# Attention scores: six bf16 part products on 99 rows, or fp32r halves in two 64-row tiles

## What is computed

```python
h = _layernorm(x) * (1 + ca) + sa
q = (h @ Wq.T); k = (h @ Wk.T); v = (h @ Wv.T)     # 32 query heads, 8 key/value heads, 16 wide
q = q * cos + _rotate_half(q) * sin; k = k * cos + _rotate_half(k) * sin
scores = einsum('bhgtd,bhkd->bhgtk', q, k) / sqrt(16)
scores = where(causal, scores, finfo.min)
attn = softmax(scores); ctx = einsum('bhgtk,bhkd->bhgtd', attn, v)
```

## Time and profile before

| | us |
|---|---|
| three runs | 859.87, 862.03 (median), 863.3 |
| the profiled execution | 858.42 |
| its span, first to last instruction | 856.4 |
| PE, DVE, ACT, POOL busy in it | 751.3, 494.3, 322.4, 217.8 |
| first score product, first transposed scores, first output projection work | 65.6, 111.7, 388 |
| one head of the loop (from one `mod_step` to the next) | 35.74 |

### The profile page before, as it was taken

The page is one execution under the profiler, slowest core; times in us unless marked ns, Lnnn a source line. Parts: engine busy times, 40 slices in busy tenths (PEclk is TensorE's granted clock), DMA queues, the critical chain, the costliest instruction groups (busy, mean ns, idle before and its releaser), DMA issues.

```text
span 856.4 us, 11611 instructions
## 1 busy us (share of the span) xinstructions
PE 751.3 (88%) x3950; PEld 462.8 (54%) x3950; DVE 494.3 (58%) x726; ACT 322.4 (38%) x533; POOL 217.8 (25%) x167
## 2 busy tenths in 40 slices
PE   3678599999999999989979999887778899997998
PEld 1565233343333433217658888644346688885886
DVE  5858876767667676406845537793686423336310
ACT  6121046555665556762315511254213322332100
POOL 2546461200000000161236523231323122222500
PEclk9789789999999999999989999998779899999999
DMA  9057893610010101211013300110221011111110
GB/s 319 10 117 104 162 181 114 81 64 21 42 63 0 63 21 42 90 38 62 2 25 102 106 1 1 33 59 1 38 65 36 25 50 49 49 35 39 62 62 37
DMA packets 24377, 52.88 MB, mean 62 GB/s; under 512 B 4017, under 2 KB 8857, under 8 KB 23321
## 3 DMA queue, kind: packets, MB, share of 16 engines
q1 hardware_dynamic: 24345, 52.46, 23.6%
HBM read 45.63 MB, written 6.62 MB: 61 GB/s over the span
## 4 chain that ended last, share of the span: by engine, by line
PE 74%; DVE 14%; issue 5%; ACT 3%; DMA 2%; POOL 2%; SPq 1%; ACTq 0%; DVEq 0%; POOLq 0%
PE ps L843 72%; DVE mxp L1716 3%; DVE xnb L1599 1%; ACT pr L1406 1%; PE ps L860 1%; DVE arena L1611 1%; DVE arena L1608 1%; DMA wm<-in_wm 1%; DVE st L1577 1%; PE ps L1002 1%; DMA Qst<-mparts 1%; DVE dg L1947 1%; DVE rt L1905 1%; POOL rs L2068 0%; POOL hrs L2252 0%
## 5 line engine op out<-in xcount | busy, mean ns | idle before, releaser
L843 PE MATMUL ps<-arena 128*128 128x512 f32 (+1 forms) x1560 | 373.2, 400 | 26.2 <-DVE arena L1611 18.3
L843 PEld LDWEIGHTS ps<-arena 128*128 128x128 f32 (+1 forms) x1560 | 296.4, 191 | 95.4 <-DVE arena L1611 25.6
L1716 DVE TENSOR_REDUCE mxp<-ps 128x2 f32<-128x1024 f32 (+3 forms) x160 | 173.1, 1116 | 68.5 <-PE ps L843 67.5
L1406 ACT ACTIVATE pr<-ps 128x512 f32<-128x512 f32 x288 | 161.7, 596 | 124.7 <-PE ps L843 122.1
L843 PE MATMUL ps<-Kst,Qst 96*128 (+4 forms) x384 | 102.1, 338 | 11.9 <-DVE full L1736 6.0
L843 PE MATMUL ps<-Qst,Kst 99*128 (+1 forms) x288 | 105.1, 386 | 8.2 <-ACT pr L1406 4.3
L843 PE MATMUL ps<-pr,vr 128*32 128x512 f32 x576 | 76.7, 605 | 0.7 <-ACT pr L1406 0.7
L843 PEld LDWEIGHTS ps<-Kst,Qst 96*128 (+1 forms) x384 | 36.1, 100 | 75.4 <-issue 34.0
L843 PE MATMUL ps<-maskb,identb 128*128 128x128 bf16 (+1 forms) x320 | 75.0, 257 | 0.0
L843 PEld LDWEIGHTS ps<-Qst,Kst 99*128 (+1 forms) x288 | 27.1, 97 | 77.3 <-ACT pr L1406 49.8
L2151 POOL COPY vr<-vtok 128x128 f32 (+1 forms) x8 | 2.3, 292 | 205.4 <-PE ps L843 205.4
(11 more groups left out here) (187 smaller groups left out, 779.3 us busy)
## 6 DMA issues: line engine op xcount, KB each, us to landing
wmr<-in_wmr SPq DMA_DIRECT2D x8, 1280.0 KB, 5.8
raw<-in_w SPq DMA_DIRECT2D x16, 512.0 KB, 3.3
Qst<-q_parts SPq DMA_DIRECT2D x18, 256.0 KB, 8.8
q_parts<-qparts SPq DMA_DIRECT2D x3, 768.0 KB, 8.5
x<-in_x SPq DMA_DIRECT2D x8, 256.0 KB, 6.1
wm<-in_wm SPq DMA_DIRECT2D x4, 512.0 KB, 7.0
raw<-in_up SPq DMA_DIRECT2D x8, 256.0 KB, 2.7
raw<-in_down SPq DMA_DIRECT2D x8, 256.0 KB, 2.6
```

The lines of the kernel that those rows point to most:

```text
L843: return nc.tensor.matmul(outp, lhs, rhs, start=start, stop=stop, skip_group_check=True)
L1406: A(pr[:, k % PRING, :], ps[:, 4 + k % 2, :], ACT.Exp, scale=float(DH) ** -0.5).then_inc(exp_done, 1)
L1716: V.tensor_reduce(mxp[:, kh, g0:g0 + heads, i].rearrange("p (b e) -> p b e", e=per), units, AXX, ALU.max)\
```

## The change

The scores are computed from fp32r halves. A stack holds hi·hi, hi·lo and lo·hi, 48 rows of 16 each. Plain scores read rows 64 to 111 of the new `Qst` and `Kst`, transposed scores rows 0 to 49 (48 and two rows of minus the maxima, as fp32r halves). The two kinds thus lie in different 64-row tiles of PE's array. Stacks are held for two heads instead of eight, and SP streams them: per head five DMAs into the upper rows and five into the lower. Loops over heads are unrolled. A unit is issued product by product (`s_piece`) among the transposed units, and ahead of `pv_round` where it stood behind. Masks are two 64-row bf16 products for a bank instead of one 128-row product for a block. Projections are plain fp32 from unsplit operands (`h0T`, `wkv`, `wq`): one product instruction a chunk instead of three. Five jobs come before the first scores; five (`FILL`) in halves behind units 0 to 9 of head 0, two later.

```diff
-KROWS = 6 * DH
+SROWS, TROWS = 3 * DH, 3 * DH + 2
+S0 = 64
...
+FILL = (("v", 1), ("q", 1, 0), ("q", 1, 1), ("q", 2, 0), ("q", 2, 1))
+VT_AT = 11
...
+    def unit(d, s):
+        heads = SUNITS[s][2]
+        for e in range(heads):
+            todo.append(("s", d, (s, e), reduce_cost(s) / heads))
...
-        Qst = at("Qst", [99, NKV, G, T], BF16, ACT_B)
-        Kst = at("Kst", [99, NKV, T], BF16, ACT_B + 65536)
+        Qst = at("Qst", [P, 2, G, T], F32R, ACT_B)
+        Kst = at("Kst", [P, 2, T], F32R, ACT_B + 32768)
...
+        maskb = at("maskb", [P, 5, 64], BF16, ACT_B + 81920 + 7168)
+        h0T = at("h0T", [P, KC, T], F32, ACT_B + 40 * 1024)
+        wq = at("wq", [P, KC, D], F32, ACT_B + 56 * 1024)
...
+        qsw = [at(f"qsw{c}", [P, T], F32, WR_B + (12 + 4 * c) * 1024)[:, :] for c in range(1, 4)]
+        qacc = at("qacc", [P, T], F32, WR_B + 28 * 1024)
+        qparts = at("qparts", [P, 2, T], F32R, WR_B + 40 * 1024)
...
+            def load_keys(base, n, tok_, done):
+                s = n % 2
+                sp.dma_start(Kst[base:base + 2 * DH, s, tok_].bitcast(F32), kscr[:, DH * n:DH * n + DH, tok_]).then_inc(done, 16)
+                sp.dma_start(Kst[base + 2 * DH:base + 3 * DH, s, tok_].bitcast(F32), kscr[0, DH * n:DH * n + DH, tok_]).then_inc(done, 16)
+            def load_queries(base, n, tok_, done):
+                s = n % 2
+                r = G * DH * (n % 2)
+                hi, lo = [qscr[n // 2, q, r:r + G * DH, tok_].rearrange("(g d) t -> d g t", d=DH) for q in range(2)]
+                for k in range(2):
+                    sp.dma_start(Qst[base + DH * k:base + DH * k + DH, s, :, tok_].bitcast(F32), hi).then_inc(done, 16)
+                sp.dma_start(Qst[base + 2 * DH:base + 3 * DH, s, :, tok_].bitcast(F32), lo).then_inc(done, 16)
+            every = slice(0, T)
+            sp.wait_ge(kst_ones, 1)
             for hf in range(2):
-                for n in (2 * hf, 2 * hf + 1):
-                    store_parts(n)
-                stored(2 * hf)
-                load_keys(0, 2, tok[hf], k_in[hf])
-                stored(2 * hf + 1)
-                load_queries(0, tok[hf], q0_in[hf])
-            load_keys(2, NKV, slice(0, T), k_rest)
-            def later_queries(c):
-                sp.wait_ge(part_q, c)
-                sp.dma_start(qscr[c, :, :, :].rearrange("q p t -> p q t"), qparts[:, :, :]).then_inc(q_out, 16)
-                sp.wait_ge(q_out, 16 * c)
-                load_queries(c, slice(0, T), q_in[c])
-            filled(sp, ("q", 3, 1))
-            sp.dma_start(wmr[:, :, :].rearrange("p c n -> p (c n)"), a["wmr"][0]).then_inc(wmr_in, 16)
-            later_queries(1)
-            def head_dmas(h, more):
+                sp.wait_ge(k_lo, hf + 1)
+                sp.dma_start(kscr[:, :, tok[hf]].rearrange("q p t -> p q t"), parts[2 * hf][:, :, :].bitcast(F32)).then_inc(part_out[2 * hf], 16)
+                sp.wait_ge(q_lo, hf + 1)
+                sp.dma_start(qscr[0, :, :, tok[hf]].rearrange("q p t -> p q t"), parts[2 * hf + 1][:, :, :].bitcast(F32))\
+                    .then_inc(part_out[2 * hf + 1], 16)
+                sp.wait_ge(part_out[2 * hf], 16)
+                load_keys(S0, 0, tok[hf], s0_in[hf])
+                sp.wait_ge(part_out[2 * hf + 1], 16)
+                load_queries(S0, 0, tok[hf], s0_in[hf])
+            for n in range(2):
+                if n:
+                    load_keys(S0, n, every, s_in[n])
+                    load_queries(S0, n, every, s_in[n])
+                load_keys(0, n, every, t_in[n])
+                load_queries(0, n, every, t_in[n])
...
+            for h in range(NKV):
+                head_dmas(h)
+                if h < 3:
+                    sp.wait_ge(part_q, h + 1)
+                    sp.dma_start(qscr[h + 1, :, :, :].rearrange("q p t -> p q t"), qparts[:, :, :].bitcast(F32)).then_inc(q_out, 16)
+                if h < NKV - 2:
+                    sp.wait_ge(q_out, 16 * ((h + 2) // 2))
+                    load_keys(S0, h + 2, every, s_in[h % 2])
+                    load_queries(S0, h + 2, every, s_in[h % 2])
+                if 1 <= h < NKV - 1:
+                    sp.wait_ge(t_full, h * NTU)
+                    load_keys(0, h + 1, every, t_in[(h + 1) % 2])
+                    load_queries(0, h + 1, every, t_in[(h + 1) % 2])
...
+            def project(name, hf, w, fresh=False, chunks=range(KC)):
+                b = bank_of(pe, name) if chunks[0] == 0 else banks.get(name)[0]
+                for kc in chunks:
+                    if fresh:
+                        evacuated(pe, ("ln", 0, hf, kc))
+                    last = mm(ps[:, b, :], w[:, kc, :], h0T[:, kc, tok[hf]], kc == 0, kc == KC - 1)
+                if chunks[-1] == KC - 1:
+                    last.then_inc(full_b[b], 1)
...
+            pe.wait_ge(wkv_in, 16)
             keys(0)
+            pe.wait_ge(wq_sorted, KC)
+            queries(0, 0)
             ln_turn(0, 1)
-            values(0)
-            weights(pe, ("wqkv", 1))
-            queries(0, 0)
-            ln_split(pe, 0, 1)
             keys(1)
             queries(0, 1)
-            values(1)
-            queries(1, 0)
-            queries(1, 1)
-            queries(2, 0)
-            def s_unit(h, s):
+            values(0)
...
+            Z = maskb[:, 0:3, :].rearrange("p a b -> p (a b)")
+            low, all_low = maskb[:, 3, :], maskb[:, 3:5, :].rearrange("p a b -> p (a b)")
+            def s_piece(h, s, e):
                 slot = s % 2
                 i, g0, heads, kh = SUNITS[s]
                 w = width(i, kh)
-                before = slots_before(h, s)
-                if not isinstance(before, int) or before >= 2:
-                    pe.wait_ge(s_read, before - 1)
+                if e == 0:
+                    before = slots_before(h, s)
+                    if before >= 2:
+                        pe.wait_ge(s_read, before - 1)
                 diag = kh == (0 if i < 4 else 1)
                 per = min(heads, 512 // w)
-                for e in range(heads):
-                    o = ps[:, 2 * slot + e // per, w * (e % per):w * (e % per) + w]
-                    last = mm(o, Qst[0:KROWS, bass.ds(h, 1), g0 + e, i * P:(i + 1) * P]
-                              .rearrange("p n t -> p (n t)"),
-                              Kst[0:KROWS, bass.ds(h, 1), 512 * kh:512 * kh + w].rearrange("p n t -> p (n t)"),
-                              True, not diag)
-                    if diag:
-                        last = mm(o[:, w - P:w], identb[:, :], maskb[:, 0, :], False, True)
-                last.then_inc(s_full, 1)
+                b = 2 * slot + e // per
+                last = mm(ps[:, b, w * (e % per):w * (e % per) + w],
+                          Qst[S0:S0 + SROWS, h % 2, g0 + e, i * P:(i + 1) * P],
+                          Kst[S0:S0 + SROWS, h % 2, 512 * kh:512 * kh + w], e % per == 0, not diag)
+                if diag and e % per == per - 1:
+                    o = ps[:, b, 0:per * w].rearrange("p (e w) -> p e w", w=w)
+                    mm(o[:, :, w - P:w], Z[S0:P, 64:192], all_low[S0:P, :].unsqueeze(1).to_broadcast([64, per, P]),
+                       False, False)
+                    last = mm(o[:, :, w - 64:w], Z[S0:P, 0:P], low[S0:P, :].unsqueeze(1).to_broadcast([64, per, 64]),
+                              False, True)
+                if e == heads - 1:
+                    last.then_inc(s_full, 1)
+            def s_unit(h, s):
+                for e in range(SUNITS[s][2]):
...
+                    pe.wait_ge(t_in[n % 2], 80 * (n // 2 + 1))
+                    pe.wait_ge(mrow_in, 32 * n + 32)
+                if k >= 2 or n > 0:
                     pe.wait_ge(exp_done, n * NTU + k - 1)
                 o = ps[:, 4 + k % 2, :].rearrange("p (g t) -> p g t", g=G)
-                last = mm(o, Kst[:, bass.ds(n, 1), j * P:(j + 1) * P].rearrange("p n t -> p (n t)"),
-                          Qst[:, bass.ds(n, 1), :, i * P:(i + 1) * P].rearrange("p n g t -> p (n g) t"),
-                          True, i > j)
+                last = mm(o, Kst[0:TROWS, n % 2, j * P:(j + 1) * P], Qst[0:TROWS, n % 2, :, i * P:(i + 1) * P], True, i > j)
                 if i == j:
-                    last = mm(o, identb[:, :], maskb[:, 1, :].unsqueeze(1).to_broadcast([P, G, P]), False, True)
+                    mm(o[:, :, 0:64], Z[0:64, 64:192], maskb[0:64, 4, :].unsqueeze(1).to_broadcast([64, G, 64]), False, False)
+                    last = mm(o, Z[0:64, 0:P], all_low[0:64, :].unsqueeze(1).to_broadcast([64, G, P]), False, True)
                 last.then_inc(t_full, 1)
...
+            pe.wait_ge(s0_in[0], 80)
             for s in range(NS):
                 if s == LATER:
-                    queries(2, 1)
+                    pe.wait_ge(s0_in[1], 80)
+                s_unit(0, s)
+                if s < 2 * len(FILL):
+                    job, half = FILL[s // 2], range(2 * (s % 2), 2 * (s % 2) + 2)
+                    if job[0] == "v":
```

(38 more changed lines are left out.)

400 lines of the change are left out of this document (148 added, 252 removed).

## The result

| | kernel before | changed kernel |
|---|---|---|
| median of the runs, us | 862.18 (859.87 to 863.3) | 946.42 (943.04 to 974.14) |
| ratio, 95% interval | | 1.0966 (1.0932 to 1.1) |
| profiled execution, span us | 856.4 | 944.6 |
| granted clock over the span | 0.944 | 0.873 |

A forecast was written before the change was run, and what follows sets the result against it. PE was taken to bound the heads (busy 33.54 of 35.74 us). Terms -13.7 - 31.2 - 2.5 + 0.8 + 13 = -33.6 took the profiled 858.4 to 824.8; predicted median 826, range 799 to 866.

The forecast's parts named there:

- the full overlap: Heads: each transposed product hides beside a plain one, 4.0 - 8.6 - 0.6 = -5.2 us, a head of 30.5 us.
- a clock of 1.00: Heads: TensorE's clock taken as unchanged from the kernel before; no term of the sum for it there.
- A new wait: Start of head 1's body: query group 2's later store delays POOL's group 3, so DVE stands 12 us; +13.
- The start: Before head 0's transposed scores: first scores at 45.5, first transposed at 98 instead of 111.68, -13.7 us.
- The forecast hold: Start of head 1's body: DVE stands 12 us waiting for POOL's query group 3.
- the +13: Head 1's body: 12 us of DVE wait, less 2, plus 3 for a fallen TensorE clock; ends 0 and 18.
- Bodies 0 to 5 gain 6 x 5.2: First six head bodies: each 5.2 us shorter, 31.2 us in all.
- the waits between them stay: Heads: PE-DVE waits, 2.2 us of PE idle a head plus about 2 in modelled ends, do not change.
- rival 3: Heads: overlap is good but hand-offs take it back, 33.5 us a head instead of 30.5; 847 us, chance 0.12.
- the +0.8 of body 7: Last head: nothing to overlap, so it pays its masks, 0.8 us.
- body 6, forecast at -2.5: Head body before the last: only 14 units beside it, so it gains 2.5 us.
- Rival 1: Heads: the tiles do not overlap, bodies 0 to 6 each +4.0 us at least; median 889 us, chance 0.20.

The follow-up runs named there:

- e1: Changed kernel with the LoRA load issued before head 0's stores instead of behind head 3's transposed stacks; 921.73 us (1.0675).
- e3: Changed kernel with the LoRA load issued before head 0's stores and query groups 1 and 2 stored earlier; 903.03 us (1.0532).
- g1: f4 with VectorE's reductions over a quarter of the columns and an exp factor of 1e-6; 842.31 us.
- g2: Kernel before with VectorE's reductions over a quarter of the columns and an exp factor of 1e-6; 850.33 us.
- e4: e3 with the last head's transposed products over 128 rows instead of 50, the added ones zero in one operand; 887.76 us (1.0334).
- f4: e4 with `pv_round` moved from behind the plain pieces back ahead of them; 879.96 us (1.0252).
- c1: Kernel before with the plain fp32 projections, their job order and `FILL`, score part left old; 853.68 us (0.991).
- b1: Kernel before, head loops written out, both kinds of score products over 48 rows in bf16 instead of 99 and 96, one row tile; 1100.29 us.

## Why the prediction was wrong

By size, three steps of the forecast failed: the full overlap in the heads; a clock of 1.00 carried over without a reason; and a second hold that "A new wait" left out. The start and the first hold came near.

**The start was right in its sum, in part by luck.** First scores 40.28 (forecast 45.5), first transposed scores 98.51 (forecast 98): -13.2 us for -13.7. That they came no earlier, though the first scores gained 25 us, is what was argued: jobs and VectorE's units stand between. But that stretch took 58.2 us for the 52.5 forecast, and the first scores were 5.2 early; the two misses cancel.

**The forecast hold was right in place and cause**, 11.4 us of VectorE for 12. Taking it out was worth 21.4 alone and, beside e1, 18.7 (921.73 - 903.03): the +13 was some 6 to 8 us too small, and of these the low clock of the held head (0.72, for 0.96 in e3) is the likely part.

**A second hold was missed.** I counted what the store of query group 2 was moved past on SP, and not the LoRA load that stands in the same loop: before it was issued at 151.36, now it is at 194.86, behind the transposed stacks of head 3, whose load waits for TensorE. GpSimd's in-order queue then held `head_v(2)`. It cost 24.7 us, which no term of the sum has. The step that failed is "A new wait": I followed one of two DMAs that changed their place.

**"Bodies 0 to 5 gain 6 x 5.2" failed, in its full-overlap step.** The prices in it were right: 0.24 alone, 0.125 for 128 columns, and a pair at 0.23. What was wrong is that a head is a stream. At full clock a head takes 37.07, +1.3 against 35.74 instead of -5.2:

- With VectorE's reductions short, a head gains 1.0 (g1, g2), not 5.2. Of the difference of 4.2, the dearer change of mode is 0.12 to 0.16 x 9 rounds = 1.1 to 1.4. The rest is argued only: between two rounds stand two to four pairs, of which one waits for an exp (transposed products then start 0.49 us apart).
- VectorE's long reductions cost 3.0 for 1.4, and by e3's head at 1.00, with the round in its other place, 37.07 - 33.40 = 3.7. In the chain of that head VectorE's reductions have 18.3% of the time, 7.0% before. I had written that the waits between them stay: they do not when the engine ahead of them changes its pattern. This was rival 3; its mechanism was right, and its price of 3 us a head is somewhat above the 1.6 to 2.3 measured (3.0 or 3.7, less 1.4), but it leaves out the 4.2 above.

**The clock of the heads was in no rival.** I had read 1.00 in the heads and carried it over, as I did for the +0.8 of body 7; the sum puts the change of clock at nothing there. Body 7 became 19.0 us longer; 15.3 of these (46.23 - 30.90) are the clock's by e4, and 3.7 are left for the 0.8 forecast. In the heads 0.91 to 0.96 costs 1.5 to 3 us each (37.07, 38.6, 40.1 in e3), and body 6, forecast at -2.5, is at 0.76 and 11.4 longer.

**Rival 1**, the one on the slow side, named a mechanism that did not happen: the tiles overlap. The forecast failed outside all its cases, and that rival 1 had the sign right is chance.

**Summed up** by medians: 43.4 us holds (946.38 to 903.03), 15.3 the clock of the last head (to 887.76), 7.8 the order of pieces (e4 to f4, not clear of the scatter), and 19.6 left in f4 above the kernel before (879.96 - 860.38, the median of that kernel beside it). If the start's gain of 7.5 (c1) lies inside that rest, the score part itself costs some 27 us even then.

**Open.** What tips the clock in heads 0 to 6: no run gave these heads full rows and kept the overlap. In e3's head of 40.14 us the clock stands at 1.00 up to 240 us and at 0.50 from 241 to 247, from the turn of the maxima on, ahead of which TensorE stood still for 0.97 us. The head ahead of it has the same order and the same pause at 1.00 throughout, and the kernel before has a pause of 1.30 us there, also at 1.00. So neither the pause alone nor the rows alone decide it. Whether the values of the operands play a part: in b1 parts of the scores are left out; in e4 the added rows are zeros, and the clock rose all the same. What the last head's other 3.7 us are was not traced.
